# Moving seven stages of a software-pipelined kernel by one or two slots, and another table for who adds the mean

## The reference

```python
x0 = x;  x = (x - mean) / sqrt(var + 1e-5)          # per image and channel
y = conv2d(x, w)                                    # 7x7, dilation 5, 32 channels -> 1
imp = sigmoid(gelu(y * scale + shift))              # one importance per pixel
idx = sort(top_k(imp, 192))                         # per image
tokens = (x * imp)[idx] + positions[idx]
t1 = layernorm(tokens + attention(tokens))          # 8 heads of 4
t2 = layernorm(t1 + feed_forward(t1))
out = x0 + where(pixel in idx, t2, x * imp)
```

## Time and profile before

| | us |
|---|---|
| median of 3 runs | 1147.99 |
| lowest and highest | 1147.3, 1151.05 |
| the profiled execution | 1148.79 |
| its span, first to last instruction | 1146.8 |
| busy PE / DVE / ACT / POOL | 932.2 / 844.7 / 766.6 / 640.5 |
| one group cycle (30 slots) when all stages overlap | 119.1 |
| mean granted TensorE clock | 0.913 |

### The profile page before, as it was taken

How to read it: one execution, slowest core, us unless ns; L and a number is a source line. 1 busy time by engine, 2 the same in 40 slices (tenths; PEclk the granted TensorE clock), 3 DMA queues, 4 the chain that set the end, 5 groups by cost and what they waited for, 6 DMA issues and landing times.

```text
span 1146.8 us, 21660 instructions
## 1 busy us (share of the span) xinstructions
PE 932.2 (81%) x6440; PEld 736.8 (64%) x6440; DVE 844.7 (74%) x2123; ACT 766.6 (67%) x1898; POOL 640.5 (56%) x845
## 2 busy tenths in 40 slices
PE   3887977499878997989798989797877698389767
PEld 2665655377657776777686868675765476377544
DVE  5345779369768996898789978996798588456644
ACT  2445654277658785968687878776778487378544
POOL 5332234742576576657775677657565764762542
PEclk9988989799989998999999999999999599789755
DMA  9997978576566999899898989975756457448779
GB/s 241 309 275 230 278 222 243 137 185 164 149 165 156 262 261 238 245 251 268 232 285 230 265 240 284 252 216 151 203 163 161 126 156 197 127 127 228 223 227 277
DMA packets 176675, 247.88 MB, mean 216 GB/s; under 512 B 65936, under 2 KB 72432, under 8 KB 176560
## 3 DMA queue, kind: packets, MB, share of 16 engines
q1 hardware_dynamic: 168368, 244.11, 76.8%
q0 software_dynamic: 8192, 2.40, 1.4%
HBM read 124.59 MB, written 121.83 MB: 215 GB/s over the span
## 4 chain that ended last, share of the span: by engine, by line
PE 36%; DVE 23%; POOL 12%; issue 10%; DMA 9%; ACT 8%; SPq 1%; DVEq 0%; POOLq 0%; ACTq 0%
PE cv L527 10%; PE sc L649 6%; PE xb L511 4%; PE pp L662 4%; POOL tok_x L1014 3%; POOL tok_imp L1014 3%; PE tr L561 3%; DVE res L1362 3%; POOL tok_pos L1014 3%; DVE stats L1131 2%; ACT wgt L846 2%; DVE junk L1150 2%; DMA X<-in_x 2%; PE ib L574 2%; DMA tok_pos<-in_pos,idx 2%
## 5 line engine op out<-in xcount | busy, mean ns | idle before, releaser
L527 PE MATMUL cv<-X,w_conv 128*128 128x330 f32 (+1 forms) x1024 | 295.8, 415 | 29.3 <-POOL X L988 27.9
L527 PEld LDWEIGHTS cv<-X,w_conv 128*128 128x128 f32 x1024 | 187.9, 198 | 63.3 <-issue 21.5
L846 ACT ACTIVATE wgt<-ib,eps_col,mom 128x440 f32<-128x440 f32 (+1 forms) x256 | 178.0, 703 | 35.1 <-DVE res L1362 23.3
L511 PE MATMUL xb<-cst,X 128*110 128x128 f32 x900 | 149.9, 292 | 39.2 <-ACT xt L812 24.4
L1051 POOL TENSOR_SCALAR res<-res,mom 128x440 f32<-128x440 f32 x144 | 97.4, 679 | 138.3 <-DVE res L1362 136.7
L649 PE MATMUL sc<-k_b,qm 128*128 128x192 f32 x768 | 162.7, 337 | 13.1 <-DVE pixf L1250 7.5
L1150 DVE TENSOR_SCALAR_CACHE_REDUCE junk<-flat,th 128x385 bf16<-128x385 f32 x200 | 122.1, 611 | 61.7 <-ACT th L832 60.5
L812 ACT COPY xt<-xb 110x512 f32<-110x512 f32 x225 | 131.7, 585 | 39.7 <-PE xb L511 27.2
L877 ACT ACTIVATE pr<-sc,least 128x192 f32<-128x192 f32 x384 | 136.8, 416 | 31.1 <-DVE least L1319 30.5
L1362 DVE SCALAR_TENSOR_TENSOR res<-tr,mom,wgt 128x440 f32<-128x440 f32 (+1 forms) x192 | 121.8, 640 | 39.9 <-PE tr L561 24.3
L1131 DVE BATCH_NORM_STATS2 stats<-X 128x6 f32<-128x458 f32 (+3 forms) x256 | 139.3, 573 | 6.4 <-DMA X<-in_x 6.3
(11 more groups left out here) (172 smaller groups left out, 1568.5 us busy)
## 6 DMA issues: line engine op xcount, KB each, us to landing
table<-xt SPq DMA_DIRECT2D x240, 224.0 KB
rt<-table SPq DMA_DIRECT2D x240, 224.0 KB
out<-res SPq DMA_DIRECT2D x320, 137.5 KB
X<-in_x SPq DMA_DIRECT2D x64, 412.5 KB, 6.4
X<-in_x SPq DMA_DIRECT2D x64, 343.8 KB, 6.4
conv_rows<-cvr SPq DMA_DIRECT2D x64, 188.0 KB
y<-conv_rows SPq DMA_DIRECT2D x64, 165.4 KB
out<-res SPq DMA_DIRECT2D x64, 68.8 KB
```

The costliest lines, as they stand in the source:

```text
L511: last = nc.tensor.transpose(bank[0:H, 128 * r:128 * r + 128], X[:, (NB * g + b) % XI, H * k:H * k + H], ident)
L527: last = mm(cv[:, 0:CUT[half]], w_conv[:, 4 * q + z], X[:, m % XI, at0:at0 + CUT[half]], start=z == 0, stop=z == 3)
L846: last = A(wgt[:, n % 2, at0:at0 + w], ib[:, at0:at0 + w], ACT.Identity, scale=mom[:, NB * g + b, 2:3], bias=eps_col[:, 1:2])
```

## The change

Seven entries of the table of slots move, and the letters of `MEAN_ON` change. No operation is added or dropped.

```diff
-        LOAD, INTO, MOMENTS, NORMAL = -21, -11, -5, (-2, -1, -1)
+        LOAD, INTO, MOMENTS, NORMAL = -21, -11, -5, (-1, -1, -1)
         TAPS, SUM = (10, 17, 25, 31), (15, 20, 28, 33)
-        GELU, IMP_OUT, FLAT, SEARCH, IMP_IN = 33, 35, 38, 40, 58
+        GELU, IMP_OUT, FLAT, SEARCH, IMP_IN = 33, 35, 38, 39, 58
         MASKS, SCANS, RANKS, HOT, PICK, INDEX = 65, 66, 68, 70, 72, 72
-        REST, SPLIT, PARTS_OUT = 78, (88, 89, 90), 92
+        REST, SPLIT, PARTS_OUT = 76, (89, 91, 91), 93
-        SCATTER, BACK, IMPB = 124, 129, (125, 129, 137, 144)
+        SCATTER, BACK, IMPB = 125, 130, (125, 129, 137, 144)
-        MEAN_ON = "PPADADPPPPPPPPDADADADAPPPPPPPP"
+        MEAN_ON = "PPPPADPPPPPPAPDPDADDDADPPADDPP"
```

## The result

The changed kernel takes 1154.32 us (median of 20 runs, 1147.2 to 1161.72), the kernel before 1147.61 us beside it. The ratio is 1.0065, with a 95% interval of 1.0045 to 1.0085: slower by 0.65%, or 7.5 us. The forecast was 1152, slower. The size was near; most of the way to it was not, as the experiments show.

The account below looks back on a forecast made before the run. No engine bounds the whole: DVE paces places 3 to 14, then POOL's gathers, then mostly PE. Terms 5.1 + 1.0 - 1.35 - 1.2 + 0.8 - 0.3 = +4.0 us gave a median of 1152, range 1141.5 to 1161.5.

Parts of the forecast that it names:

- term 3: Scans of `find_greater` beside POOL: still held by a longer run; with the search's end +0.35 each in groups 3 to 5.
- terms 4 and 5: Late places and added slot: POOL's additions taken away -1.2, DVE's new ones +0.8, slot 0, ACT's one less -0.3.
- Term 1: Places 23 and 24: gathers end earlier, convolution starts later, PE's clock falls; 0.85 for each of six windows, +5.1 us.
- Rival A: Scans of `find_greater` escape POOL's run: 1.8 to 2.5 us gained per group in groups 2 to 5, time 1143.5; chance 0.2.
- The sign that I had named: Scans of L1180 or L1185 keep a maximum near 3.6 us or more; none above 1.5 us means wrong.
- Term 2: Places 3 and 4, end of the search: DVE loses about 1.3 us, so slot 6 starts about 1.2 us earlier.
- Rival C: PE's lower clock lasts through slots 24 to 26: +2.5 for six windows, 15 in place of 5, time 1162; chance 0.13.
- Rival B: Nothing is left of gain or loss: clock loss 0.8 and not 1.7 us, time 1147; chance 0.25.

Follow-up runs that it names:

- the kernel with term 1 alone: Kernel before with part 0 of the normalisation at one slot ahead for all images (`NORMAL = (-1, -1, -1)`): 1146.16 us, ratio 0.9972.
- the one with the fourth image back: Changed kernel with part 0 of the normalisation two slots ahead for the fourth image alone (place 21, between the gathers): 1158.7 us, ratio 1.0114.
- one letter alone: Kernel before with one letter of `MEAN_ON` changed, place 22's addition on DVE in place of POOL: 1160.54 us, ratio 1.0098.
- 1145.67: Kernel before with `NORMAL = (-1, -1, -1)` and the search one slot earlier (`SEARCH = 39`): 1145.67 us, ratio 0.9984.
- the short ones: Changed kernel with DVE's additions of the mean at places 15 to 22 cut to 8 columns of 440: 1146.05 us, ratio 0.9977.

## Why the prediction was right, and where it was not

Right in size (1154.3 against 1152, inside the range) and in sign, but by luck in the main: the scans (term 3) and the way back with its letters (terms 4 and 5) were each wrong by some 8 to 9 us, in opposite directions, and cancelled.

**Term 1 (the normalisation), +5.1 forecast.** At its own place it held: with this change alone PE waited 4.24 us, the clock fell, and places 14 to 24 of groups 0 to 5 together grew by 4.1 us in the trace (1.6 to 1.9 in groups 0, 1 and 4, 0.6 in group 3, nothing in group 5, and 1.7 less in group 2). Its tokens waited 3.99 us and not 2.3: the lag, which I had kept at 1.84, was 3.9, as the gathers ended 2.7 us earlier while the DMA engines were still at a share of 0.63. But the whole of this change measured -3.2 us, not +5.1, for what follows.

**Term 3 (the scans), the step that failed.** "DVE reaches the scans at 612.95", and POOL's first X at 613.2: a margin of 0.25 us. It is 1.03 (620.56 and 621.59 above). Counted from the start of slot 6, both sides of the sum were off. POOL was later: its X starts 5.20 us behind it, where I had 4.9, for its first scatter starts 1.37 behind it and not 0.6, and power and copies took 1.5 where I had 1.3, while the two DMAs between took 2.3 where I had 3.0. DVE was earlier: its scans start 4.17 behind it, where I had 4.65. One reason is that the mask (L1174) took 0.62 us, and 1.13 in the kernel before, where a normalisation ran on POOL beside it. In the kernel with term 1 alone the two figures are the same (5.20 and 4.18). A forecast that hangs on a quarter of a microsecond between two sums of six terms should have had even chances. Rival A had 0.2. Its price was right per cycle (1.8 to 2.5 forecast, 2.6 at place 8, of which 0.55 is given back at places 9 to 13 in the kernel with term 1 alone). The sign that I had named came out against me: no scan of L1180 is above 0.85 us and none of L1185 above 1.23.

**Term 2, -1.3 us on DVE.** The time did leave DVE, but the threshold's matmul came no sooner: 11.6 us behind the start of slot 4 (604.42 to 616.02), against 11.3 before (10.8 and 10.5 behind the start of the taps' sum). PE no longer waits for DVE at L581 (1.10 before), but 2.00 us for ACT's copy at the start of slot 5, which had been 1.37:

```profile
611.08 0.65 PE L511 MATMUL xb<-cst,X 128*110 128x128 f32 x4 [2.00 <-ACT xt L812]
...
616.02 0.27 PE L581 MATMUL tr<-tsel,cst 128*110 128x4 f32 x2
```

In ACT's order that copy stands behind gelu and exp, each with a table load of 1.28 us, and gelu waits for the taps' sum, so slot 5 starts as late as before (6.66 us behind slot 4, where it was 6.77):

```profile
605.09 1.28 ACT L836 ACT_TABLE_LOAD   x1
606.82 0.76 ACT L836 ACTIVATE ge<-yy,wts 110x440 f32<-110x440 f32 x1 [0.44 <-DVE yy L1267]
```

What took the gain is TensorE's clock behind that wait. Slot 5 in the windows, of the kernel before, of the changed one, and of the one with the fourth image back, with PE at L581 of the last:

```profile
604.52:609.50 4.98, 3.87 (x25) 3.12 (x26) 4.84 (x10) 3.90 (x10) 2.97 (x6) 1.00 0.70 186
```

```profile
611.08:616.39 5.31, 5.31 (x26) 4.54 (x27) 4.38 (x8) 3.69 (x9) 2.62 (x3) 0.68 0.49 137
```

```profile
611.03:614.79 3.76, 3.75 (x25) 3.12 (x26) 3.73 (x7) 3.76 (x9) 1.98 (x2) 1.00 0.33 97
...
614.34 0.35 PE L581 MATMUL tr<-tsel,cst 128*110 128x4 f32 x2
```

PE does in 5.31 us, without a gap and at a granted clock of 0.68, what took it 3.87 at 1.00. In the third kernel the wait was the same (1.99 us), the clock stayed at 1.00 in this group, and the matmul came 9.95 us behind the start of slot 4: 1.35 sooner than in the kernel before, much what term 2 had forecast. In groups 2 and 3 of the changed kernel the clock was 0.69 there, so they lose it too. The step that failed is that term 2 priced DVE's time alone and left the clock out at this place, though it had it in term 1. The wait alone does not decide: behind 1.38 us in group 4 of the kernel with term 1 alone the clock was 0.68 as well.

**Terms 4 and 5, forecast at -0.7 together: the large miss.** At the late places they held (2.52 and 2.82 us against 2.0 and 3.1). What was missed is the steady cycle. I costed the letters as work on POOL, ACT and DVE, and the slot of `BACK` as one slot at the end; I did not ask which store waits for which letter, and so where SP stands. Alone, the letters cost 17 us and the slot 16, and one letter alone 11. In the changed kernel these, with `split` and `find_rest` (not run alone), make the difference between 1145.67 and 1154.32, 8.7 us. A second part of it is the D letters beside the gathers: I had them at 0.43 us each of DVE with room to spare, and with them at full length POOL's gathers lose 3.2 us a group, in place of 0.6 with the short ones (1.7 in group 4 of the kernel before, which has three such letters and not five).

**Rival C** named the right place and the time of the slowest executions (1162), by the wrong mechanism: not the clock, but the lag. **Rival B** did not occur.

What stays open: why the later way back alone costs 16 us, when the three stretches with the long lag (the ten slots up to slots 148, 178 and 208) are together 12 us longer in its trace, and all of it 14 us; and what `split` and `find_rest` do by themselves.

## What to carry to other kernels

A wait on an issuing queue is also a brake: before moving a consumer or giving its work to a freer engine, list what the queue behind that wait would issue, and who then stands behind those transfers. A gather's cost ends at its landing, so read the share of the DMA engines between the last issue and the first use. Where two waits end within a few us of each other, an experiment that removes one of them shows little; remove both before a cause is dropped. Where time is taken off one engine, look at the granted clock of the engine that now waits for another: here 1.35 us were won by DVE and spent on PE's lower clock.

## What was not expected of the hardware

- A gather beside DVE's work can take 2.60 us in place of 0.92. The one at 672.54 met a reduction and an addition behind it, and ended at 675.14, 0.80 us after the addition (674.34); in the kernel before one of 1.92 us ended 0.79 us after the same addition, and one of 1.70 us in the changed kernel (660.28) 0.79 us after another. Two of 1.00 and 1.02 us (677.90, 669.99) ended only 0.11 and 0.12 us after theirs. Gathers beside the same reduction without a full addition behind it took 0.92. Not every gather that starts in the reduction is held: in group 2 of the kernel before one that started 0.08 us into it took 0.92. The condition isn't settled.
- Of two sets of scans beside the same run of three normalisations, the first, which began 1.03 us ahead of it, went through in 1.21 us; the second, begun inside the run, took 3.05. In the kernel before, one that began 0.51 us ahead of a run of two was held 3.3 us. So it isn't simply held "until the run is over", as I had it.
- Leaving out half of each output store moved the time of the kernel before by 0.3% and not at all that of the changed one, though in both, with whole stores, the DMA engines have a share of 0.92 over the cycle.
